# Mixture-of-experts layer: every expert on every token against tokens sorted by expert on the chip

## What is computed

```python
x = x + attn(layernorm(x))          # 16 heads of 8, masked scores, softmax
x = x + xattn(layernorm(x), ctx)    # 1601 context rows per batch
x = x + ffn(layernorm(x))

def ffn(x):                         # T = 4096 tokens, D = 128, INTER = 256, E = 8, TOPK = 2
    scores = softmax(xt @ gate_w.T)
    _, indices = top_k(scores + gate_bias, 2)
    weights = take_along_axis(scores, indices)
    combine = (one_hot(indices, 8) * weights[..., None]).sum(1)     # T x 8, two non-zero per row
    for e in range(8):
        y += mlp(xt, w1[e], w2[e], w3[e]) * combine[:, e:e+1]
    return y + mlp(xt, sw1, sw2, sw3)                               # the shared expert
# mlp(x, w1, w2, w3) = (silu(x @ w1.T) * (x @ w3.T)) @ w2.T
```

## Time and profile before

| | |
|---|---|
| median of 3 runs | 994.62 us (994.24 to 994.80) |
| the profiled execution, first to last instruction | 997.1 us |
| PE busy | 896.1 us, 90% |
| PE weight loads | 694.8 us, 70% |
| DVE | 540.2 us, 54% |
| ACT | 425.3 us, 43% |
| POOL | 289.7 us, 29% |
| mean granted TensorE clock | 0.980 of full speed |
| chain that ended last | PE 77%, ACT 5%, issue 5%, DVE 5%, POOL 3% |
| DMA | 57.49 MB |

### The profile page before, as it was taken

How to read it: one execution, slowest core, us unless ns; L and a number is a source line. 1 busy time by engine, 2 the same in 40 slices (tenths; PEclk the granted TensorE clock), 3 DMA queues, 4 the chain that set the end, 5 groups by cost and what they waited for, 6 DMA issues and landing times.

```text
span 997.1 us, 19846 instructions
## 1 busy us (share of the span) xinstructions
PE 896.1 (90%) x6528; PEld 694.8 (70%) x6528; DVE 540.2 (54%) x1291; ACT 425.3 (43%) x887; POOL 289.7 (29%) x495
## 2 busy tenths in 40 slices
PE   1697998998898899899899887789999999999998
PEld 0354766666676676676666666779888888888887
DVE  0443565475475465556547543556655555555554
ACT  1133555545645645555554564334222222222221
POOL 2235345435435524634633543242000000000000
PEclk9995999999999999999999999789999999999999
DMA  7124144134134224414413411000000000000000
GB/s 237 32 51 105 42 112 128 34 99 123 40 99 116 58 82 116 93 52 111 126 34 101 124 36 58 9 1 1 2 11 1 11 11 0 11 11 0 11 11 11
DMA packets 64282, 57.49 MB, mean 58 GB/s; under 512 B 5872, under 2 KB 57984, under 8 KB 64128
## 3 DMA queue, kind: packets, MB, share of 16 engines
q1 hardware_dynamic: 64256, 57.15, 21.8%
HBM read 45.20 MB, written 11.53 MB: 57 GB/s over the span
## 4 chain that ended last, share of the span: by engine, by line
PE 77%; ACT 5%; issue 5%; DVE 5%; POOL 3%; SPq 1%; DMA 1%; POOLq 0%; DVEq 0%; ACTq 0%
PE banks L194 20%; PE banks L203 13%; PE banks L653 7%; PE banks L610 7%; PE banks L588 4%; PE banks L636 4%; PE banks L590 3%; PE banks L691 3%; POOL prob L1142 3%; PE banks L581 2%; PE banks L583 2%; ACT prob L862 2%; DVE xmax L984 2%; PE banks L717 1%; PE banks L672 1%
## 5 line engine op out<-in xcount | busy, mean ns | idle before, releaser
L268 ACT ACTIVATE prob<-banks 128x512 f32<-128x512 f32 x144 | 86.0, 598 | 228.1 <-PE banks L194 178.7
L306 DVE TENSOR_TENSOR prob<-banks,prob 128x512 f32<-128x512 f32 x144 | 99.3, 691 | 107.0 <-ACT prob L268 106.9
L203 PEld LDWEIGHTS banks<-w_sb,prob 128*128 128x128 f32 x1152 | 139.1, 192 | 6.0
L203 PE MATMUL banks<-w_sb,prob 128*128 128x128 f32 x1152 | 140.4, 275 | 0.0
L194 PE MATMUL banks<-x_hi,w_hi 128*128 (+1 forms) x288 | 120.7, 419 | 0.1
L653 PE MATMUL banks<-info,xprobT 128*128 128x128 f32 (+1 forms) x832 | 108.3, 282 | 9.6 <-ACT xprobT L838 9.6
L976 DVE TENSOR_REDUCE mx<-banks 128x2 f32<-128x512 f32 x128 | 87.3, 683 | 50.8 <-PE banks L590 50.7
L194 PE MATMUL banks<-x_lo,w_hi 128*128 (+1 forms) x288 | 114.3, 397 | 0.0
L862 ACT ACTIVATE prob<-banks 128x512 f32<-128x512 f32 x192 | 99.8, 617 | 32.4 <-PE banks L676 32.4
L194 PE MATMUL banks<-x_hi,w_lo 128*128 (+1 forms) x288 | 113.6, 394 | 0.0
L653 PEld LDWEIGHTS banks<-info,xprobT 128*128 128x128 f32 (+1 forms) x832 | 100.0, 195 | 17.2 <-ACT xprobT L838 17.2
(11 more groups left out here) (143 smaller groups left out, 1388.3 us busy)
## 6 DMA issues: line engine op xcount, KB each, us to landing
infoT<-in_ctxT SPq DMA_DIRECT2D x16, 800.5 KB, 5.8
info<-in_ctx SPq DMA_DIRECT2D x16, 768.0 KB
kst<-k_stack SPq DMA_DIRECT2D x32, 192.0 KB
q_parts<-parts SPq DMA_DIRECT2D x32, 96.0 KB, 2.3
k_stack<-parts SPq DMA_DIRECT2D x32, 96.0 KB, 2.3
qst<-q_parts SPq DMA_DIRECT2D x32, 96.0 KB
w_raw<-in_w SPq DMA_DIRECT2D x16, 144.0 KB, 5.5
k_stack<-parts SPq DMA_DIRECT2D x32, 64.0 KB, 2.1
```

What stands on the lines that cost most here:

```text
L203: mm = pe.matmul(ps[:, Y_BANKS[n], t * D:(t + 1) * D], lhsT=h[n][z][:, t * P:(t + 1) * P], rhs=w2_sb[:, e, z, :], start=(z == 0), stop=(z ...
L268: act.activation(sil[z], ps[:, 2 * z, :], ACT.Silu).then_inc(s["silu_done"], 1)
L306: dve.tensor_tensor(h[n][z], ps[:, 2 * z + 1, :], sil[z], ALU.mult).then_inc(s["h_done"], 1)
```

## The change

The routed experts no longer run over all tokens. Each token is written twice to a DRAM buffer, once in the region of each expert it chose; the buffer is then read back in 72 tiles of 128 rows, each tile belonging to one expert.

- In the batch loop. The steps get two more batches each: `rte` (batch l = i-3) does the third layer norm, its transposes, the rounding of the transposed tokens, the gate product, the softmax and the top-2 choice for that batch; `pos` (batch o = i-4) computes each token's place in its expert's region (a triangular matmul counts the tokens ahead of it, `filled` carries the count over) and POOL scatters four tiles of 128 rows of 520 bytes (features, weight, home row) by indirect DMA. Steps 2 and 3 are unrolled, and two steps follow at the end (18 and 19).
- `beside`, `shared_step` and the `trans`, `norm`, `stats` parts are gone. The 8 units of the shared expert all run before the routed ones, after DVE's `slots()`, which computes the expert and the start of each of the 72 tiles; SP meanwhile pads each region to whole tiles.
- The routed part is 36 pairs of tiles, written out without a loop. Tokens are now stationary and weights moving. Per pair PE does 6 matmuls of 512 columns with the expert's number out of a register, 4 transposes of the hidden rows, 4 matmuls of 128 columns; per two pairs 4 transposes of tokens; per pair two register loads (`value_load`). ACT and DVE round, gate and copy; ACT multiplies by the token's weight.
- POOL scatters each finished tile by indirect DMA to a DRAM array with one row per token and choice. When all 72 are written, SP reads both halves of that array back (16 DMAs of 256 KB), DVE adds them to `xall`, and SP writes the output.

The core of the diff:

```diff
+            def sorted_up(q):
+                g = q // 2
+                if q % 2 == 0:
+                    pe.wait_ge(s["sx_lo"], g + 1)
+                if q >= 2:
+                    pe.wait_ge(s["shid_done"], q - 1)
+                for t in range(2):
+                    of = bass.ds(expert[2 * q + t], 1)
+                    c = slice((2 * (q % 2) + t) * P, (2 * (q % 2) + t + 1) * P)
+                    for n, (a, b) in enumerate(((xT_hi, w13_hi), (xT_lo, w13_hi), (xT_hi, w13_lo))):
+                        mm = pe.matmul(ps[:, UP_BANKS[q % 2] + t, :], lhsT=a[g % 2][:, c], rhs=b[:, of, :].rearrange("p o n -> p (o n)"),
+                                       start=(n == 0), stop=(n == 2))
+                mm.then_inc(s["sup_ps"], 1)
...
+                pe.wait_ge(s["slots_done"], 1)
+                experts_of(0)
+                sorted_x(0)
+                pe.wait_ge(s["shared_done"], NGR)
+                for q in range(PAIRS):
+                    if q + 1 < PAIRS:
+                        experts_of(q + 1)
+                    sorted_up(q)
+                    if q % 2 == 0 and q // 2 + 1 < PAIRS // 2:
+                        sorted_x(q // 2 + 1)
+                    if q >= 1:
+                        sorted_hT(q - 1)
+                    if q >= 2:
+                        sorted_down(q - 2)
+                sorted_hT(PAIRS - 1)
+                sorted_down(PAIRS - 2)
+                sorted_down(PAIRS - 1)
...
+            def sorted_y(q):
+                act.wait_ge(s["sy_ps"], q + 1)
+                for t in range(2):
+                    j = 2 * q + t
+                    if j >= 8:
+                        act.wait_ge(s[f"home{j % 8}"], 16 * (j // 8))
+                    act.activation(routed[j % 8], ps[:, Y_BANKS[q % 2], t * D:(t + 1) * D], ACT.Copy,
+                                   scale=sorted_in[(q // 2) % SB][:, 2 * (q % 2) + t, D:D + 1]).then_inc(s["sy_sb"], 1)
...
+                base, at = cst[0:1, C_REG:C_REG + E], cst[0:1, C_AT:C_AT + SLOTS]
+                number = cst[0:1, C_SLOT:C_SLOT + SLOTS].unsqueeze(2).to_broadcast([1, SLOTS, E])
+                dve.wait_ge(s["filled_set"], B + 1)
+                dve.tensor_copy(pad_at[:], filled[0:1, :]).then_inc(s["slots_done"], 1)
+                final(1, dve.scalar_tensor_tensor(tiles_i[:], filled[0:1, :], float(P - 1), base, ALU.add, ALU.subtract))
+                final(2, dve.tensor_scalar(tiles_i[:], tiles_i[:], 7, None, ALU.logical_shift_right))
+                final(3, dve.tensor_copy(tiles_f[:], tiles_i[:]))
+                final(4, dve.tensor_tensor_scan(tiles_end[:], cst[0:1, C_ONE:C_ONE + E], tiles_f[:], 0.0, ALU.mult, ALU.add))
+                final(5, dve.tensor_tensor(past, number, tiles_end[:].unsqueeze(1).to_broadcast([1, SLOTS, E]), ALU.is_ge))
+                final(6, dve.tensor_tensor(past_n, past, tiles_f[:].unsqueeze(1).to_broadcast([1, SLOTS, E]), ALU.mult))
+                final(7, dve.tensor_reduce(slot_e[:], past, AX.X, ALU.add))
+                final(8, dve.tensor_reduce(slot_b[:], past_n, AX.X, ALU.add))
+                dve.tensor_copy(expert_i[:], slot_e[:]).then_inc(s["slots_done"], 1)
+                final(9, dve.scalar_tensor_tensor(slot_at[:], slot_e[:], float(REGION), at, ALU.mult, ALU.add))
+                dve.scalar_tensor_tensor(from_i[:], slot_b[:], float(-P), slot_at[:], ALU.mult, ALU.add).then_inc(s["slots_done"], 1)
...
+            def sorted_home(j):
+                g = j // GT
+                pool.wait_ge(s["sy_sb"], j + 1)
+                pool.indirect_dma_start(dy, bass.IndirectOffsetOnAxis(ap=sorted_in[g % SB][:, j % GT, D + 1:D + 2].bitcast(I32), axis=0),
+                                        routed[j % 8], None, bounds_check=LAST - 1, oob_is_err=False
+                                        ).then_inc(s[f"home{j % 8}"], 16)
...
+            for g in range(SLOTS // GT):
+                if g >= SB:
+                    for j in range(GT * (g - SB), GT * (g - SB + 1)):
+                        sp.wait_ge(s[f"home{j % 8}"], 16 * (j // 8 + 1))
+                for t in range(GT):
+                    j = GT * g + t
+                    at = sp.value_load(from_i[0:1, j:j + 1], min_val=0, max_val=SORTED - P)
+                    sp.dma_start(sorted_in[g % SB][:, t, :], dsort[bass.ds(at, P), :]).then_inc(s[f"in{g % SB}"], 16)
+            for n in range(8):
+                sp.wait_ge(s[f"home{n}"], 16 * (SLOTS // 8))
+            home_tiles = dy[0:DUMP, :].rearrange("(k t p) d -> p k t d", k=TOPK, p=P)
+            for g in range(NGR):
+                for k in range(TOPK):
+                    sp.dma_start(back[k][:, GT * g:GT * g + GT, :], home_tiles[:, k, GT * g:GT * g + GT, :]).then_inc(s[f"back{g}"], 16)
             out_tiles = out.rearrange("b (t p) d -> p (b t) d", p=P)
-            with sp.Fori(0, NGR) as g:
-                apart(sp, "acc_done", GT * E * g + GT * E)
-                sp.dma_start(out_tiles[:, bass.ds(GT * g, GT), :], xall[:, bass.ds(GT * g, GT), :]).then_inc(s["out_done"], 16)
+            for g in range(NGR):
+                sp.wait_ge(s["sum_done"], 2 * g + 2)
...
+                if pos:
+                    pe.wait_ge(s["picked"], o + 1)
+                    pe.wait_ge(s["tri_done"], 2)
+                    first = oh_bf[:, 0, :].unsqueeze(1)
+                    pe.matmul(ps[:, 7, 0:2 * E], lhsT=tri_bf[:], rhs=oh_bf[:].rearrange("p t e -> p (t e)"),
+                              start=True, stop=False, skip_group_check=True)
+                    pe.matmul(ps[:, 7, E:3 * E].rearrange("p (c e) -> p c e", c=2), lhsT=ones_bf[:], rhs=first.to_broadcast([P, 2, E]),
+                              start=False, stop=False, skip_group_check=True)
+                    pe.matmul(ps[:, 7, 2 * E:3 * E], lhsT=ones_bf[:], rhs=oh_bf[:, 1, :],
+                              start=False, stop=True, skip_group_check=True).then_inc(s["rank_ps"], 1)
...
+                if pos:
+                    pe.wait_ge(s["rank_read"], 3 * o + 1)
+                    pe.wait_ge(s["filled_set"], o + 2)
+                if rte:
+                    pe.wait_ge(s["xn3_done"], 2 * l + 2)
+                    for t in range(T):
+                        mm = pe.transpose(ps[:, 7, S + t * P:S + (t + 1) * P], xn3[:, t, :], ident)
+                    mm.then_inc(s["xn3T_ps"], 1)
...
+                if rte:
+                    act.wait_ge(s["shifted"], l + 1)
+                    act.activation(ex[:], biased[:], ACT.Exp).then_inc(s["ex_done"], 1)
...
+                def choose(n, k):
+                    route(n, dve.tensor_reduce(best[:], biased[:], AX.X, ALU.max))
+                    route(n + 1, dve.tensor_tensor(eq[:], biased[:], wide(best), ALU.is_equal))
+                    route(n + 2, dve.tensor_tensor(eq[:], eq[:], by_expert(C_IOTA), ALU.mult))
+                    route(n + 3, dve.tensor_reduce(ind[:], eq[:], AX.X, ALU.max))
+                    route(n + 4, dve.tensor_tensor(oh[:, :, k, :], by_expert(C_IOTA), wide(ind), ALU.is_equal))
+                def route_scores():
+                    if not rte:
+                        return
+                    dve.wait_ge(s["lg_sb"], l + 1)
+                    route(1, dve.tensor_reduce(lmax[:], logit[:], AX.X, ALU.max))
+                    dve.tensor_tensor(biased[:], logit[:], wide(lmax), ALU.subtract).then_inc(s["shifted"], 1)
+                def route_choices():
+                    if not rte:
+                        return
+                    dve.wait_ge(s["ex_done"], l + 1)
+                    route(2, dve.tensor_reduce(esum[:], ex[:], AX.X, ALU.add))
+                    route(3, dve.reciprocal(erec[:], esum[:]))
+                    route(4, dve.tensor_tensor(sc[:], ex[:], wide(erec), ALU.mult))
+                    route(5, dve.tensor_tensor(biased[:], sc[:], by_expert(C_GB), ALU.add))
+                    choose(6, 0)
+                    route(11, dve.scalar_tensor_tensor(biased[:], oh[:, :, 0, :], NEG, biased[:], ALU.mult, ALU.add))
+                    choose(12, 1)
+                    if pos:
+                        apart(dve, "rank_ps", l)
+                    dve.tensor_tensor(oh_bf[:], oh[:, :, 0, :], oh[:, :, 1, :], ALU.add).then_inc(s["picked"], 1)
+                    route(17, dve.tensor_tensor(ohw[:], oh[:], by_choice(sc), ALU.mult))
+                    if pos:
+                        apart(dve, "sent", 64 * l)
+                    route(18, dve.tensor_reduce(row[:, :, :, D].rearrange("p k t -> p t k"), ohw[:], AX.X, ALU.add))
+                def places():
+                    if not pos:
+                        return
+                    dve.wait_ge(s["rank_ps"], o + 1)
+                    dve.wait_ge(s["filled_set"], o + 1)
+                    dve.tensor_tensor(rank[:], ps[:, 7, 0:T * E].rearrange("p (t e) -> p t e", t=T),
+                                      filled[:].unsqueeze(1).to_broadcast([P, T, E]), ALU.add).then_inc(s["rank_read"], 1)
```

(29 more changed lines are left out.)

527 lines of the change are left out of this document (270 added, 257 removed).

## The result

The changed kernel takes 1019.4 us (median; 1013.0 to 1020.9) where the kernel before takes 994.7 us on the same chip: ratio 1.0234, 95% interval 1.0203 to 1.0264. It is 2.3% slower. The forecast was 970 us, range 912 to 1035. The time is inside the range and the sign is wrong.

What follows compares the result with a forecast made beforehand. The prediction took PE to bound the routed part and the DVE stretch from heads_out(0) to q_lo to lie on every batch step's path. Shared experts' start 799.3 + 42 + 104 + 27 = 972.3, hence 970 us, range 912 to 1035.

Steps and rivals of the forecast that it cites:

- 36 x 2.8 + 3 us of filling = 104 us: Routed part: 36 pairs of tiles at 2.8 us, set by POOL's two scatters, against 293.4 us before.
- Wrong: pairs over 3.5 us with POOL's queue full or PE idle ahead of up: Routed part: signs against the forecast, a full POOL queue meaning rival 2, PE idle meaning stalls on register loads.
- rival 2: Routed part: POOL's scatters set the pace, slower than before from 1.75 us each; 1019 us at 2.08; chance 0.20.
- rival 4: Routed part: matmuls at half clock because PE waits in each pair; 43 us more, 1013 us; chance 0.04.
- Down: 4 + 4 instructions of 0.111: Routed pair on PE: 4 + 4 matmuls or transposes of 128 columns, 0.89 us of PE's 2.51 us.
- Scatters on POOL: Routed part: two indirect DMAs a pair on POOL, 1.4 us each, bounds 0.38 and 2.08 us.
- Batch steps, +10.0 us forecast: Each batch step grows from 36 to about 46 us by four terms; +127 us over steps 3 to 15.
- (a): Batch step: the top-2 choice, 17 chained DVE instructions between heads_out(0) and the additions; +3.2 us.
- (b): Batch step: POOL's instructions hold up the choice's two-input DVE instructions; +4.2 us, bounds 0 and +5, q_lo gaining 0.9.
- (c): Batch step: places() stands first on DVE, waits for a matmul and delays what feeds PE; +3.3 us.
- (d): Batch step: gate product and two more transposes on PE where it has no gap; +0.2 us.
- Rival 1: Batch steps: DVE and POOL don't block each other, q_lo keeps its 1.34 us; 41 us less, 929 us; chance 0.18.

Runs made afterwards that it cites:

- e9: Changed kernel with a ring of six tile groups instead of four, run again on the third chip; 969.0 us.
- e12: The changed kernel as it is, run again on the third chip; 1009.6 us.
- e1: Changed kernel with a ring of six tile groups instead of four, first chip; 968.4 us, ratio to before 0.9722.
- e4: Changed kernel, ring of four, with the top-2 choice ahead of the cross attention's reciprocal and ACT's exp ahead of its first group; 923.4 us.
- e7: Changed kernel with one wait added: POOL, from the second info_lo on, waits for the top-2 choice's last instruction; 982.7 us.
- e5: Changed kernel with choice moved as in e4, plus places() behind the next row's normalised input and POOL's four scatters behind `on`; 902.6 us.
- e10: Changed kernel with all three edits (ring of six, choice ahead, places moved), the program of e6 run again on the third chip; 859.1 us.
- e3: Changed kernel with ring of six and each tile's expert a constant instead of a register loaded by PE; 969.8 us.
- e6: Changed kernel with all three edits: ring of six, choice ahead, places moved; second chip; 879.0 us, ratio to before 0.8835.
- e8: Changed kernel with ring of six and half of each tile's down product left out, second chip; 988.2 us.
- e11: Changed kernel with ring of six and half of each tile's down product left out, run again on the third chip; 958.6 us.

## Why the prediction was wrong, point by point

**The step that failed is the routed part, "36 x 2.8 + 3 us of filling = 104 us".** It is a sum of busy times per pair, with POOL's scatters as the beat. Nothing in it asked when a tile can be loaded. The loads were put down as lying under the shared expert, which is true of the first 16 (the ring's four groups) and of no other. The 56 that follow each wait for the scatters of the group four before, and behind a load stand its landing, the transposes, two pairs of lag on PE, ACT's output, the scatter and its landing: PE stands 26 us in eight waits and runs at the lower clock behind them. Ring of six: 41 us less on one chip (e9 against e12), and PE with next to no gap. Of the 43 us between 145.1 and 102.3 from the first to the last up, 26 are these waits; PE's busy time falls by 13.5 (115.4 to 101.9 us), as its clock goes from 0.92 to 1.00. "Wrong: pairs over 3.5 us with POOL's queue full or PE idle ahead of up" named the size; the pair is 4.15 us, but PE idles ahead of the token transposes for a DMA, a case that stood in none of the rivals. The change's diff and the value SB = 4 were enough to find it. That 1019.4 us lies in the range is luck: the upper end was there for rivals 2 and 4, and neither came about.

Against e1, where the wait is gone, the same sum holds by its terms: 788.9 us for 799.3 up to the shared expert, 41.9 for 42, 107 for 104, and 31 for 27; the span is 968.8 us for 972.3. The closeness of the total is partly luck too, since these misses cancel.

**Down: 4 + 4 instructions of 0.111.** The row itself says 16 instructions for a down with 8 matmuls in the source; I multiplied the source's 4 by 0.111. It is 8, so PE needs 2.94 us a pair and not 2.51. This was hidden by the next term and costs 0.14 us a pair over the 2.8 of the sum, some 5 us with a ring of six.

**Scatters on POOL.** Priced at 1.4 us; they take 0.98 and 0.30 between two, 1.28 us. View: page, costliest groups, kernel after.

```profile
L462 POOL DMA_INDIRECT routed_out<-vaug,infoT x56 | 54.7, 977 | 112.5 <-ACT vaug L362 100.2
...
L1305 POOL DMA_INDIRECT sorted_rows<-row,place x64 | 65.0, 1015 | 24.9 <-issue 24.9
```

The value chosen between 0.38 and 2.08 was good, and rival 2 (scatters at 1.75 us or more) falls: its 1019 us was met to the microsecond by another mechanism. The second rule that the prediction takes from the Trainium skill (page "SBUF — State Buffer", section "SBUF: two separate sides"), that descriptor writing stands while DVE copies in a two-port mode, is not tested here: DVE runs only TENSOR_TENSOR in the routed part (L427 and L434, both with an input in PSUM), and no scatter into routed_out is longer than 0.99 us.

**Batch steps, +10.0 us forecast.** +9.5 us measured in the first result (45.5), +8.6 in most steps on two other chips (44.6 in e1 and e12), where the granted clock of a step is 0.92 to 0.93 instead of 0.89. By the parts: (a) and (b) together less q_lo's gain, 3.2 + 4.2 - 0.9 = 6.5; e4 takes away 5.9 to 6.8. (b) alone +4.2; e7 takes away 2 to 3, so the chain's own length was under-priced (4.5 us with POOL beside only its first half, where I had 3.9; the trace has 18 instructions, two of them overlapping, where I had 17) and POOL's hold over-priced (the longest member lasts 1.16 us, the other two-input ones 0.17 to 0.58). (c) +3.3; e5 takes away 1.6 to 1.9. The rest, about 1 us, stays in e10's 36.9 us against 36.02, so (c) was over-priced too, by half a microsecond at least. The mechanism of (a), (b) and (c) was right; (d) was not tested alone. Rival 1, DVE and POOL passing each other, falls with L1115's 1159 and 175 ns.

**Shared expert and the last steps.** 795.0 us and 41.9 us, forecast 799.3 and 42. The misses in the 795.0 nearly cancel: from the second to the fifteenth q_lo the batches took 118 us more than before (forecast 127), what comes after took 23 us more (forecast 20.5), and the first q_lo came 2.7 us later, which the forecast had at nothing.

**Register loads.** Taken as covered; e3 agrees.

**Half clock in the routed part (rival 4).** It is there (1.91 for 1.06 us), but as a consequence of the waits: with the ring of six the granted clock is 1.00.

**The end, 27 us forecast.** 32 us: POOL's last eight scatters run from 984.25 to 994.2 us back to back, five of them start after PE's last down (987.6 us), and my "3 us" did not hold that, as POOL was to be in step with PE. From SP's first read at 995.56 us on it is 23.4 us for 6.3 MB, 269 GB/s, where I had 21 us at 296.

## What to carry to other kernels

For a new pipeline, price the loop as well as the beat: a buffer's whole way from its load to the last reader that frees it, divided by the number of buffers, against the time of one stage, and include what stands behind the waiting instruction on its engine. When small dependent instructions are added to an engine, first look for a stretch in which it is idle; the same chain cost 6 us a step at one place and at most 0.9 at another (e10's 36.9 us against 36.02, with all that the change adds). And count instructions in the trace of a line of the same type, not in the source.

## What the runs showed of the hardware

One execution of an indirect DMA of 128 rows of 512 bytes takes GpSimd 0.98 us in the routed part (1.01 in the batch loop) with 0.30 us to the next, and lands 2.3 us from its issue.

ScalarE can start 0.4 to 4.4 us late behind TensorE's rows without any change in the program. The changed kernel had it in its profiled run and not in e12; e6 and e8 had it and e10 and e11, the same programs on another chip, had not. On the chip with it the tile loads on SP are uneven too. View: one line's instructions, tile loads of e6_all and of e10_all_again (ns, shortest/median/longest).

```profile
L590 SPq FUSED_REGOPS  x48: 3/37/699, 735.7 to 819.2; - x48
...
L590 SPq DMA_DIRECT2D info<-sorted_rows x24: 3/168/634, 756.8 to 819.9; - x24
```

```profile
L590 SPq FUSED_REGOPS  x48: 37/37/37, 734.7 to 802.8; - x48
...
L590 SPq DMA_DIRECT2D info<-sorted_rows x24: 332/333/342, 752.5 to 803.0; - x24
```

Where PE is the bound the routed part is 17 us longer with it (119.6 against 102.3 us from the first to the last up, e6 and e10), where the ring is the bound hardly at all (145.1 against 144.5, changed kernel and e12). It stands in the batch steps too: the score maxima (L1053, L1057) that DVE stands waiting for start 1.0 to 1.9 us behind PE's rows in 16 of 75 cases of the changed kernel, and never more than 0.6 us behind them in e12. The 10 us between the two lie there (the shared expert starts at 795.0 and at 784.6 us); the granted clock differs as well, and no run parts the two. What causes the lateness is open; no run here tells a property of the chip from one of its surroundings. It does not touch the verdict: without it the changed kernel takes 1009.6 us against 993.7, one run each, still 1.6% slower than before.
